# A reordered schedule for two grouped attentions, three ternary feed-forwards and a decayed attention, with head means folded into centred weights

## What is computed

```python
# L1A: 16 heads of 128, 4 key/value heads, gated, causal
q, k = rope(layernorm(x @ Wq, per head) * w + b), the same for k
out = softmax(q @ k.T / sqrt(128) + causal) @ v * sigmoid(x @ Wg) @ Wo
# L3A: 32 heads of 128, 4 key/value heads, causal
q, k = rope(rmsnorm(x @ Wq, per head) * w), the same for k
out = softmax(q @ k.T / sqrt(128) + causal) @ v @ Wo
# L2A: 16 heads of 16, linear attention with decay, rms norm, @ Wo
# L1F, L2F, L3F (hidden 1024), act_quant = int8 rounding with a scale per token, ternary weights
h = silu(act_quant(x') @ W1) * (act_quant(x') @ W2)
y = act_quant(h') @ W3
# L1F: x', h' are rms-normed with gains; L2F: biases; L3F: h' is the Hadamard transform of h
```

## Time and profile before

| | |
|---|---|
| median of 3 runs | 3810.17 us (3807.21 to 3814.23) |
| profiled execution | 3804.77 us, span 3803.0 us |
| PE busy | 3030.0 us, 80% |
| DVE busy | 2608.3 us, 69% |
| ACT busy | 1856.9 us, 49% |
| granted TensorE clock, mean | 0.872 |

### The profile page before, as it was taken

The page is one execution under the profiler, slowest core; times in us unless marked ns, Lnnn a source line. Parts: engine busy times, 40 slices in busy tenths (PEclk is TensorE's granted clock), DMA queues, the critical chain, the costliest instruction groups (busy, mean ns, idle before and its releaser), DMA issues. The chain is left out here.

```text
span 3803.0 us, 55008 instructions
## 1 busy us (share of the span) xinstructions
PE 3030.0 (80%) x16888; PEld 2200.9 (58%) x16888; DVE 2608.3 (69%) x8195; ACT 1856.9 (49%) x5724; POOL 475.3 (12%) x589
## 2 busy tenths in 40 slices
PE   7985554979999998864489865599999999998565
PEld 5653333747777777641266642277777777777344
DVE  4658886358888887667755478676666666665686
ACT  4546764125555554445422124366666666655232
POOL 0012120011111111211111110111111111111100
PEclk9996556989999999975599876799999999999587
DMA  1004655000000000001100121100000000000011
GB/s 60 1 25 84 105 103 150 1 15 1 1 1 1 1 1 11 32 32 22 39 1 1 46 108 28 28 1 1 1 1 1 1 1 1 1 1 33 2 23 45
DMA packets 192417, 96.23 MB, mean 25 GB/s; under 512 B 186112, under 2 KB 190336, under 8 KB 190464
## 3 DMA queue, kind: packets, MB, share of 16 engines
q1 hardware_dynamic: 192128, 92.73, 10.0%
HBM read 44.47 MB, written 2.10 MB: 12 GB/s over the span
## 5 line engine op out<-in xcount | busy, mean ns | idle before, releaser
L2321 DVE CUSTOM_DVE_ANT_0 L3A_masked<-ps,L3A_hidden,L3A_negrstd 128x128 f32<-128x128 f32 (+1 forms) x512 | 193.7, 415 | 322.0 <-PE ps L2212 230.3
L2270 ACT ACTIVATE L3A_probs<-L3A_masked,L3A_negmax 128x128 f32<-128x128 f32 (+1 forms) x512 | 228.7, 449 | 237.7 <-DVE L3A_negmax L2321 237.4
L336 PE MATMUL ps<-s_weights_b,s_XT 128*128 128x512 f32 (+1 forms) x640 | 298.9, 597 | 30.1 <-ACT L1A_qn L2128 8.3
L2240 PE MATMUL ps<-s_weights_b,L3A_OT 128*128 128x256 f32 x1024 | 265.0, 382 | 14.2 <-DVE s_R L2350 14.2
L2193 POOL TENSOR_TENSOR L3A_rstd<-L3A_ve,s_mhalf 128x4 f32<-128x4 f32 x144 | 145.0, 1007 | 851.1 <-DVE L3A_ve L2153 851.1
L336 PE MATMUL ps<-s_weights_b,s_Xc 128*128 128x512 f32 x512 | 245.1, 601 | 7.4 <-DVE L3A_rot L2185 3.3
L885 ACT ACTIVATE L0X_pf<-ps,L0X_bias,L0X_qscale 128x512 int16<-128x512 f32 x256 | 197.0, 777 | 90.7 <-DVE L0X_bias L918 90.2
L336 PEld LDWEIGHTS ps<-s_weights_b,s_XT 128*128 128x128 f32 x640 | 121.9, 209 | 121.3 <-issue 72.0
L2240 PEld LDWEIGHTS ps<-s_weights_b,L3A_OT 128*128 128x128 f32 x1024 | 175.1, 191 | 28.6 <-issue 15.4
L915 DVE TENSOR_REDUCE L0X_negmax<-ps 128x2 f32<-128x1024 f32 x128 | 156.1, 1219 | 35.6 <-PE ps L826 35.0
L2270 ACT ACTIVATE L1A_probs<-L1A_masked,L1A_negmax 128x128 f32<-128x128 f32 (+1 forms) x256 | 114.3, 447 | 120.3 <-DVE L1A_negmax L2321 117.5
(11 more groups left out here) (512 smaller groups left out, 8366.7 us busy)
## 6 DMA issues: line engine op xcount, KB each, us to landing
s_weights_b<-w_L3A SPq DMA_DIRECT2D x1, 9984.0 KB, 26.7
s_weights_b<-w_L1A SPq DMA_DIRECT2D x1, 7936.0 KB, 21.7
s_weights_a<-w_L2F SPq DMA_DIRECT2D x1, 4224.0 KB, 13.1
s_weights_b<-w_L1F SPq DMA_DIRECT2D x1, 3840.0 KB, 11.7
s_weights_b<-w_L3F SPq DMA_DIRECT2D x1, 3136.0 KB, 11.0
s_weights_a<-w_L2A SPq DMA_DIRECT2D x1, 2898.0 KB, 11.1
s_weights_a<-w_L0F SPq DMA_DIRECT2D x1, 2176.0 KB, 9.7
s_X<-x SPq DMA_DIRECT2D x1, 2048.0 KB, 8.4
```

The costliest lines, as they stand in the source:

```text
L336: last = pe.matmul(out, lhs(k), rhs(k), start=(k == 0), stop=(k == n - 1))
L2240: last = pe.matmul(c.bank(3)[:, j * DM:(j + 1) * DM], OT[:, u % 4, j * P:(j + 1) * P], w["wo"][:, h, :], start=(h == 0 and j == 0), stop=( ...
L2270: last = a.activation(pr[:, u % 4, cols], ms[:, u % 2, cols], ACT.Exp, bias=nmx[:, h, j:j + 1], scale=-1.0, accum_out=sm[:, h, j:j + 1])
L2321: last = eng.tensor_tensor_reduce(out=ms[:, u % 2, cols], in0=s[:, cols], in1=hidden[:, P - j * P:2 * P], scale=-1.0 if gated else nrs[:, ...
```

## The change

It has four parts.

1. **Grouped attentions.** PE's `part` moves from `s-5` to `s-6`; `take_out` from `s-4` at the end of a step to `s-5` at its start (ACT in L3A, DVE in L1A); ACT's `take_probs` stands ahead of `exps`; DVE's `add_parts` moves one step later and to the front of its step. In L3A query rotations are made in the step of their projection (keys one step after it), and now wait for the squares of that step; their halves are transposed 3 steps after the slot instead of 5. Slots and gate slots change, one step is added.
2. **L1A statistics.** DVE centres the key and query weights in SBUF once, per group (`vec_centre`). The head mean is then zero: `bn_stats`, `bn_aggr` and `nmr` go, and ACT's squares give the variance as in L3A.
3. **Ternary feed-forwards.** `LAG` is 5; `silu` comes first in ACT's step and `round_hidden` moves from the end of step `s` (tile `s-2`) to the middle of the next one (`s-3`); `gate_times_up` comes first in DVE's step, ahead of `norm`; L2F has a third buffer of `h`. In L1F a few one-column operations are merged.
4. **L2A.** PE transposes rows straight from `X`; the copies go.

```diff
-    LAG = 4
+    LAG = 5
+    HB = 3 if kind == "L2F" else 2
...
                 if norms:
                     square_input(0)
-                for s in range(NT + 3):
+                for s in range(NT + 4):
+                    if 1 <= s <= NT:
+                        silu(s - 1, 0)
+                        silu(s - 1, 1)
                     if norms and s + 1 < NT:
                         square_input(s + 1)
                     if s < NT:
                         round_input(s)
...
+                    if 3 <= s < NT + 3:
+                        round_hidden(s - 3)
...
-    slots = {1: -7, 2: -2, 3: 2, 4: 6, 5: 10, 6: 13, 7: 16, 8: 19, "K": -10, "V": -4}
+    slots = {1: -7, 2: -1, 3: 2, 4: 5, 5: 9, 6: 12, 7: 16, 8: 19, "K": -10, "V": -4}
...
-                rotations_at.setdefault(a + 2 + j, []).append((i, g, j))
+                rotations_at.setdefault(a + j + (2 if gated else 1 if g == "K" else 0), []).append((i, g, j))
...
-                early.setdefault(a + (4 if gated else 5) + b, []).append(("half", i, g, b))
+                early.setdefault(a + (4 if gated or g == "K" else 3) + b, []).append(("half", i, g, b))
...
+        def vec_centre(v, g):
+            e = v.eng
+            part = w["wk"] if g == "K" else w["wq"][:, :, (g - 1) * 512:g * 512]
+            for k in range(KC):
+                v(e.tensor_reduce(cen[:, k, :], heads_of(part[:, k, :], 4), AX.X, ALU.add), free=k == 0)
+            v(e.tensor_scalar(cen[:], cen[:], 1.0 / WIDE, None, ALU.mult))
+            for k in range(KC):
+                h_ = heads_of(part[:, k, :], 4)
+                v(e.tensor_tensor(h_, h_, spread(cen[:, k, :], WIDE), ALU.subtract), centred if k else None, free=k == 0)
...
-                e.wait_ge(rows_made, TT * r + j + 1)
+                e.wait_ge(sq_ready, TT * r + j + 1)
...
-                    if 0 <= s - 5 < U:
-                        part(s - 5)
+                    if 0 <= s - 6 < U:
+                        part(s - 6)
...
-                v(eng.tensor_copy(c.Xc[:], c.X[:, TT:2 * TT, :]), S.x_copied)
...
-                        S.pe_turn_x(pe, t=b)
+                        pe_turn_rows(pe, b + 1, b)
```

More of the change, by code:

```diff
@@ L1414, in _ @@
                         round_input(s)
-                    if 1 <= s <= NT and not biases:
-                        silu(s - 1, 0)
-                        silu(s - 1, 1)
+                    if 3 <= s < NT + 3:
+                        round_hidden(s - 3)
                     if hadamard and 2 <= s < NT + 2:
@@ L1420, in _ @@
                         a.copy(flat(uT[:]), c.ps[:, 5:7, :].rearrange("p a b -> p (a b)")).then_inc(uT_ready, 1)
-                    if 1 <= s <= NT and biases:
-                        silu(s - 1, 0)
-                        silu(s - 1, 1)
-                    if s >= 3 and not hadamard:
-                        t = s - 3
+                    if s < NT:
+                        a.wait_ge(xi_turned, s + 1)
+                        a.copy(xiT[:, s % 2, :, :, :].rearrange("p q k t -> p (q k t)"),
+                               c.bank(0, BF16)[:, 0:XQ * KC * P]).then_inc(xiT_ready, 1)
+                    if 4 <= s < NT + 4 and not hadamard:
+                        t = s - 4
                         a.wait_ge(hq_turned[t % 2], 16 * (t // 2 + 1))
@@ L1584, in _ @@
                             gate_times_up(s - 1, hf)
+                    if norms and 2 <= s < NT + 2:
+                        hidden_mean(s - 2)
+                    if norms and s + 1 < NT:
+                        input_mean(s + 1)
+                    if s > LAG:
+                        norm(s - LAG - 1)
                     if s < NT:
@@ L2127, in act_norm @@
             for s in range(4):
-                last = a.activation(qn[:, j, s * P:(s + 1) * P], c.bank(j)[:, s * P:(s + 1) * P], ACT.Identity,
-                                    scale=rstd[:, j, 4 * slot(g) + s:4 * slot(g) + s + 1], bias=nmr[:, j, s:s + 1])
+                last = a.activation(qn[:, j, s * P:(s + 1) * P], c.bank(j)[:, s * P:(s + 1) * P], ACT.Copy,
+                                    scale=rstd[:, j, 4 * slot(g) + s:4 * slot(g) + s + 1])
             last.then_inc(normed, 1)
@@ L2286, in _ @@
                 for s in STEPS:
+                    if 0 <= s - 5 < U and not gated:
+                        take_out(s - 5)
                     for x in early.get(s, []):
                         act_side(a, x)
+                    if 0 <= s - 3 < U:
+                        take_probs(s - 3)
                     if 0 <= s < U:
                         exps(s)
-                    if 0 <= s - 3 < U:
-                        take_probs(s - 3)
                     for i, g, j in rows_at.get(s, []):
@@ L2295, in _ @@
                             act_take_values(a, i, j)
-                        elif not gated:
+                        else:
                             act_squares(a, i, g, j)
@@ L2300, in _ @@
                             act_norm(a, i, g, j)
-                    if 0 <= s - 4 < U and not gated:
-                        take_out(s - 4)
                     for x in late.get(s, []):
@@ L2397, in _ @@
                 for s in STEPS:
-                    for i, g, j in stats_after.get(s - (not gated), []):
+                    for i, g, j in stats_after.get(s - 1, []):
                         pool_pow(p, i, g, j)
-                    if s >= H and (s - 5) % H == 0 and s - 5 <= U:
-                        S.pool_rstd(p, (s - 5) // H - 1)
+                    if s >= H and (s - 6) % H == 0 and s - 6 <= U:
+                        S.pool_rstd(p, (s - 6) // H - 1)
         S.clear()
@@ L2435, in sublayer_l2_attn, with pe_turn_rows @@
             "scores_made", "sd_ready", "o_made", "o_ready", "var2_ready", "rs_ready")
+        def pe_turn_rows(pe, seq, t=0):
+            if t:
+                pe.wait_ge(S.y_read, t)
+            xt = c.bank(0).rearrange("p (k t) -> p k t", k=KC)
+            for k in range(KC):
+                for j in range(TT):
+                    last = pe.transpose(xt[:, k, j * P:(j + 1) * P], c.X[:, (seq + 1) * TT + j, k * P:(k + 1) * P], c.k["ident"])
+            last.then_inc(S.xT_made, 1)
         def pe_qk(pe, j, t=0):
@@ L2558, in _ @@
                 pe.wait_ge(S.loaded, 16)
[L2559 removed]
+                pe_turn_rows(pe, 0)
                 for j in range(TT):
```

156 lines of the change are left out of this document (65 added, 91 removed).

## The result

The changed kernel takes **3708.51 us** (median of 4 runs, 3698.18 to 3710.6); the kernel before took 3808.69 us in the same session (3803.55 to 3814.23). The ratio is 0.9731, with a 95% interval of 0.9708 to 0.9754: it is faster, by 100 us where I forecast 127 against the profiled execution, and the forecast's range holds it.

The account below looks back on a forecast made before the run. PE bounds L3A, L1A and L2A, loops through several engines the ternary stages; 36 + 30 + 25 + 26 + 10 + 0 = 127 us less than 3804.8 gives 3678, plus 5.4 for the median: 3683 us, range 3640 to 3735.

Parts of the forecast that it names:

- their terms: Time less forecast per stage: L1A 30 us, L1F 26, L2A 25, L2F 10.
- the sum of 26: L1F: DVE's waits of 20.8 us for silus and 8.5 for POOL's power go, less 3 us of fill.
- New holes: L3A: 0.5 us for each of 8 sequences, and 0.9 us of ACT copy for each of 7; 10 us.
- PE stays the longer by 0.2 us, so the new order works: L3A, slots three apart: three steps take PE 11.8 us and the DVE-ACT chain 11.6, so PE leads, barely.
- slots four apart [...] give slack back: L3A: argument against the rotation rival, that slots four apart and the value and key groups give slack back.
- the comparison by the sum of several steps: L3A: two rotation steps and one without, 11.6 us, set against PE's same three steps, 11.8.
- the rotation chain of L3A is just too long: Rival, chance 0.16: L3A halves wait 1 us in each of 64 groups, a third given back; +43, 3726 us.
- The loop: L3F: transform, gates, second silu, xq and hq, turn, next transform; 10.1 us at full clock, 12.8 with the slow stretch.
- transform start to gates start: Link of L3F's loop: 3.50 us where the clock is full, 6.17 at the lower level.
- the rival at the lower clock: Rival, chance 0.13: L3F's new loop takes 12.8 us and more a tile, +25 over the stage; 3708 us.
- the row of before: L2A: clock 0.91 with 1.9 us holes per batch, read as holes costing clock; 10 us expected back.
- The slower rival: Rival, chance 0.03: in L3A ACT's accumulator reads don't overlap, chain 6.2 us instead of 5.0; 141 us lost, 3824.

Follow-up runs that it names:

- the order without the chain: Changed kernel with L3A's query rotations one step after their projection and their halves at slot plus 4: 3651.06 us, ratio 0.9588.
- the kernel with both edits: Changed kernel with L3A's query rotations and halves one step later and L3F's hq back at the end of ACT's step: 3645.95 us, ratio 0.9571.

## Why the prediction came out as it did

**The forecast held in four of six stages.** L1A, L1F, L2A and L2F came within 3 us of their terms. In L1A the reason holds too: the order closed the holes, and ACT's new 59 us and the 95 us less on DVE were rightly costed at nothing. In L2F the wait for the power was 11.3 us, and its removal 8.1 to 8.2. In L1F the sum of 26 was right partly by luck: its two waits fell by 19.9 us (20.8 to 6.0, and 8.5 to 3.4), not by 26, and most of the rest of the 28.2 came from what the sum left out, 3.9 us less work on DVE (153.74 to 149.88) and 2.9 us less waiting for the squares of the rows. The two parts, measured apart, aren't additive either.

**The term that was mis-sized is L3A's: 36 us forecast, 16.6 measured.** The closed holes were priced well: `s_R`, `probsT` and 13.8 us of rotations ahead of projections are 42 us, where I had 40. PE's busy time fell by 12 us, where I had 6 for clock and small gains. New holes were put at 10 us; they are some 37: 26.7 on `L3A_OT`, 8.3 more ahead of the halves (at the start of the stage alone, not in each sequence), 5.4 for the copies of the rows, less small waits that went. The step that failed is "PE stays the longer by 0.2 us, so the new order works", with a chain of 5.0 us per rotation step. The timeline of the changed kernel over two such steps shows what the chain takes:

```profile
2703.74 0.35 DVE L2311 CUSTOM_DVE_ANT_0 L3A_masked<-ps,L3A_hidden,L3A_negrstd 128x128 f32<-128x128 f32 x1
...
2704.61 0.48 ACT L2268 COPY L3A_probsT<-ps 128x384 f32<-128x384 f32 x1
2704.98 0.41 ACT L2260 ACTIVATE L3A_probs<-L3A_masked,L3A_negmax 128x128 f32<-128x128 f32 x1
...
2705.87 0.27 ACT L2117 ACTIVATE s_oT<-ps 128x128 bf16<-128x128 f32 x1
...
2706.87 0.40 ACT L2274 COPY L3A_OT<-ps 128x256 f32<-128x256 f32 x1
2707.04 0.69 DVE L2168 TENSOR_TENSOR L3A_rot<-ps,L3A_G 128x512 f32<-128x512 f32 x1 [1.88 <-ACT s_oT L2117]
...
2709.36 0.35 DVE L2311 CUSTOM_DVE_ANT_0 L3A_masked<-ps,L3A_hidden,L3A_negrstd 128x128 f32<-128x128 f32 x1
...
2711.38 0.28 ACT L2117 ACTIVATE s_oT<-ps 128x128 bf16<-128x128 f32 x1 [0.20 <-PE ps L336]
...
2714.72 0.35 DVE L2311 CUSTOM_DVE_ANT_0 L3A_masked<-ps,L3A_hidden,L3A_negrstd 128x128 f32<-128x128 f32 x1
...
2716.27 0.35 DVE L2311 CUSTOM_DVE_ANT_0 L3A_masked<-ps,L3A_hidden,L3A_negrstd 128x128 f32<-128x128 f32 x1
```

From maxima to maxima it is 5.62 and 5.36 us, and 1.55 without a rotation: 12.5 for three steps, not 11.6, and more than PE's 11.8. Over the whole stage, 31 such threes take 12.3 us on the mean. In the first step the exponentials start 1.24 us after the maxima, not 0.80, since `probsT` now stands ahead of them; in the second the squares wait for PE's projection. So the chain was longer than PE's work by 0.5 to 0.7 us, not shorter by 0.2, and the part that I had costed at nothing, `take_probs` in the chain, is one of its links.

But PE doesn't pay for this where slots are three apart. From scores to scores, its stretches of three steps take 11.2 to 11.9 us on the mean of the sequences behind the first, and 13.1 where the next sequence's rows are transposed; with later rotations they take 11.2 to 11.9 and 13.0. It pays where slots are four apart. This is the end of such a stretch, behind the two steps with a projection (PE in the changed kernel):

```profile
2655.36 0.39 PE L2201 MATMUL ps<-L3A_kT,L3A_qT 128*128 128x128 f32 x2
...
2657.39 0.67 PE L2219 MATMUL ps<-L3A_probsT,L3A_V 128*128 128x256 f32 x2 [0.89 <-ACT L3A_OT L2274]
...
2658.99 0.39 PE L2201 MATMUL ps<-L3A_kT,L3A_qT 128*128 128x128 f32 x2
...
2661.57 0.67 PE L2219 MATMUL ps<-L3A_probsT,L3A_V 128*128 128x256 f32 x2 [1.01 <-ACT L3A_OT L2274]
...
2663.17 0.38 PE L2201 MATMUL ps<-L3A_kT,L3A_qT 128*128 128x128 f32 x2
```

These two bare steps take 3.63 and 4.18 us, where the run with later rotations has 2.94 and 2.50. On the same mean the two stretches of four steps take 17.13 and 15.95 us, and 14.32 each with later rotations: 4.4 of the 4.8 us that a whole sequence loses. So a second step of the prediction failed, "slots four apart [...] give slack back", and with it the comparison by the sum of several steps. A likely reason, which no run tests alone: a rotation step of the chain (5.62 and 5.36 us above) is longer than PE's step with a projection (4.65), so after two of them the copy of the output is late, and in the bare steps no projection of 1.9 us stands ahead of `values` to cover that.

The rival "the rotation chain of L3A is just too long" had the mechanism right but the wrong place: it put the loss on the halves, whose time holds 12 us of it, and on a slack that the fours don't give. It forecast 43 us above my number, and the stage came out 19 above. Against the order without the chain the loss is 48 us; the difference is that this order gains more than I had charged. Without the chain L3A gains 64 us (1067.8 to 1003.6), where the gains in my sum were 46; the copy of the probabilities alone is worth 22.7 there, where the waits had shown 14.1.

**L3F was put at 0 and is +4.5.** The loop is the one described, and the wait is on `hq` as said. The link that was mis-sized is "transform start to gates start", for which the sum took the mean of 3.50 us "where the clock is full" and 6.17: two tiles of the changed kernel have 6.19 and 4.93. The others fit: gates to turn 4.00 and 4.22 (forecast 4.1), turn to transform 2.17 and 2.39 (2.36). The clock has a part in it. Of the sixteen transforms five ran at the full clock in the kernel before, in 2.05 us each (one is in the earlier trace rows); in the changed kernel only the first does, and the others take 3.48 to 3.78 us at a granted clock of 0.50 to 0.57. With `hq` put back it is five again. So the rival at the lower clock is half right: behind the first tile no transform runs at full clock any more, but it forecast 12.8 us a tile and +25, and the tiles are 12.00 apart, since the clock rises within the link in every second tile (4.93 and not 6.19) and the loop of before was at 11.53 with its slow transforms. Putting `hq` back gave 5.7 us (4.4 in the kernel with both edits), so the order sets off the loss; how much of it goes through the clock no run tells.

**L2A and its clock.** The 15.1 us went, and the first wait too fell from 6.0 us to 3.8. PE's busy time fell by 6.7 us with the same 1808 matmuls, where I had 10 us for the clock; the clock went from 0.91 to 0.94, not to 0.97. The sum had read the clock wrongly by a factor of two: a mean of 0.91 over 259.5 us is 23 us of work lost and some 47 at the lower level (the trace has 44), not 12 and 23, and the 0.99 of L3A likewise. In the trace 12 of the 22 us lost lie in the loop, by luck the number that the sum used, and 5 of them stay. The loop shows where the clock stands now, in windows of the changed kernel that nearly match its batches:

```profile
1863.00:1888.00 25.00, 25.00 (x213) 19.52 (x212) 13.16 (x41) 6.03 (x12) 3.43 (x4) 0.93 0.00 1
1888.00:1913.00 25.00, 24.98 (x220) 19.80 (x219) 14.75 (x46) 6.03 (x12) 3.41 (x4) 1.00 0.01 2
...
1988.00:2013.00 25.00, 25.00 (x214) 19.56 (x213) 13.29 (x40) 6.03 (x12) 3.42 (x4) 0.93 0.01 2
```

So the holes did cost busy time, as the row of before had suggested, but two thirds of what I charged. From the first value matmul (`L2A_sd`) of one batch to that of the next it is now 24.52 us where the clock stays full and 26.07 where it falls once; before, with the hole, it was 26.49 without a fall and about 28.1 with one. Over seven batches there were seven falls before and there are three now: four falls less, at 1.55 us each, are 6.2 of the 6.7 us. But the clock still falls in three of seven batches in which the profile, whose matmul ends are modelled, shows no hole at all. What makes it fall there stays open; no run was spent on it. By the Trainium skill, "TensorE: Matmul & The Clock Gate", section "HAM oscillation", closing such holes gives back no clock; the stage gained 23.6 us, nearer to the 25 of the row than to the 15 of that rule, and the 0.93 without a hole agrees with neither.

**L3A's clock** stood at 0.98 or 0.99 in all versions, so it isn't where the 48 us went.

## What to carry to other kernels

When an instruction is moved into the step of the work that it waits for, write down the whole ring through the engines, with every instruction that now stands between, the cheap copies too, and compare it with the leading engine's time step by step, not only for the sum of several steps; a lead of 0.2 us in 12 is no lead, and here the loss fell on the steps that the sum had counted as slack. A consumer that can stand one step behind its producer should: here that was worth 36 us, and 12 more for its own consumer. In an in-order engine, first comes what the leading engine waits for; and where a part of a change only relieves an engine that has slack (the statistics of L1A), it was worth nothing here, and the run that leaves it out shows it.

## What the runs showed of the hardware that I had not expected

- TensorE's granted clock fell to 0.93 in windows of 25 us in which the profile has it busy for 25.00 us; each such fall made a batch of L2A 1.55 us longer (26.07 against 24.52).
- An ACT square with its accumulator read costs less than the sum of the two rows: ACT starts the next one after 0.25 us (2705.87 to the copy at 2706.87 for four), where the rows give 277 and 208 ns. The slower rival rested on the opposite.
- The same code of L2X took 85 to 86 or 89 us in different kernels; nothing in it was edited, and the cause stays open.
